# Transposing attention probabilities as two halves of 64 query rows, on the two row halves of TensorE and into two PSUM banks

## The reference

```python
q = l2norm(q) * qs; k = l2norm(k) * ksc
q, k = rotary_xpos(q, k)
sim = jnp.einsum('bhwid,bhwjd->bhwij', bq * 8.0, look_around(bk))   # i: 128 queries, j: 256 keys
sim = jnp.where(mask, -jnp.finfo(sim.dtype).max, sim)
attn = jax.nn.softmax(sim, axis=-1)
out = jnp.einsum('bhwij,bhwjd->bhwid', attn, look_around(bv))
x = x + o @ wo                                                      # then a gated feed-forward block
```

## Time and profile before

| | |
|---|---|
| median of 3 runs | 2342.65 us (2342.46 to 2345.71) |
| span of the profiled execution | 2341.2 us; no other time is given for that execution |
| TensorE matmuls busy | 2090.4 us (89%) |
| weight loads busy | 1569.1 us (67%) |
| DVE, ACT, POOL busy | 1155.5, 930.8, 652.2 us |
| mean granted TensorE clock | 0.938 |
| local attention, first to last score | 586.05 to 1212.4 us, with a feed-forward block between its layers |

### The profile page before, as it was taken

How to read it: one execution, slowest core, us unless ns; L and a number is a source line. 1 busy time by engine, 2 the same in 40 slices (tenths; PEclk the granted TensorE clock), 3 DMA queues, 4 the chain that set the end, 5 groups by cost and what they waited for, 6 DMA issues and landing times. The chain is left out here.

```text
span 2341.2 us, 38218 instructions
## 1 busy us (share of the span) xinstructions
PE 2090.4 (89%) x12396; PEld 1569.1 (67%) x12396; DVE 1155.5 (49%) x4116; ACT 930.8 (40%) x2973; POOL 652.2 (28%) x568
## 2 busy tenths in 40 slices
PE   8996899776999989899989979979997799599998
PEld 5764488554667745467764558758886577489997
DVE  4886244365777732377763347722221465423332
ACT  3652132233666632266663125412221466133332
POOL 0377556522122210022211002222223022213332
PEclk8997799978999999899999979979998899699999
DMA  6601299875920020100000072111220801372221
GB/s 228 267 16 35 93 322 341 234 246 160 343 104 10 9 62 0 38 10 10 10 12 1 1 257 97 36 42 31 35 38 10 288 28 35 139 253 37 36 35 19
DMA packets 155370, 232.21 MB, mean 99 GB/s; under 512 B 36585, under 2 KB 123604, under 8 KB 154262
## 3 DMA queue, kind: packets, MB, share of 16 engines
q1 hardware_dynamic: 125750, 201.55, 24.7%
q0 software_dynamic: 29424, 28.21, 6.8%
HBM read 142.88 MB, written 101.04 MB: 104 GB/s over the span
## 5 line engine op out<-in xcount | busy, mean ns | idle before, releaser
L3058 POOL TENSOR_TENSOR la_invnorm<-la_clamped,all_minushalf 128x16 f32<-128x16 f32 x32 | 92.9, 2903 | 372.7 <-DVE la_clamped L3123 372.7
L2679 ACT ACTIVATE m3e_ht<-m3e_h_bank,m3w_b 128x128 f32<-128x128 f32 x312 | 89.1, 369 | 188.8 <-PE m3e_h_bank L2652 188.8
L3205 ACT ACTIVATE la_probs<-la_probs,la_nb,la_invnorm 128x256 f32<-128x256 f32 x256 | 150.1, 591 | 5.1 <-DVE la_nb L3145 5.1
L2652 PE MATMUL m3e_h_bank<-m3e_xt,m3e_w 128*128 128x128 f32 x1248 | 147.4, 277 | 0.0
L2624 POOL DMA_INDIRECT out<-m3e_y,m3e_dest x39 | 82.0, 2102 | 225.4 <-DVE m3e_y L2724 223.4
L2652 PEld LDWEIGHTS m3e_h_bank<-m3e_xt,m3e_w 128*128 128x128 f32 x1248 | 144.3, 194 | 0.1
L2663 PE MATMUL m3e_y_bank<-m3w_w,m3e_ht 128*128 x624 | 141.0, 379 | 0.0
L881 POOL DMA_INDIRECT m_xbuf<-m0w_rows,m0w_slots x128 | 127.8, 998 | 37.5 <-issue 36.0
L2843 ACT ACTIVATE m2e_ht<-m2e_h_bank,m2w_b 128x270 f32<-128x270 f32 x128 | 62.2, 487 | 178.7 <-PE m2e_h_bank L2808 178.6
L2783 POOL DMA_INDIRECT m_sum<-m2e_y,m2e_dest x48 | 70.2, 1463 | 199.3 <-DVE m2e_y L2891 193.8
L2663 PEld LDWEIGHTS m3e_y_bank<-m3w_w,m3e_ht 128*128 128x128 f32 x624 | 115.7, 190 | 14.1
(11 more groups left out here) (486 smaller groups left out, 4806.0 us busy)
## 6 DMA issues: line engine op xcount, KB each, us to landing
m0w_wgu<-in_m_gu SPq DMA_DIRECT2D x32, 768.0 KB, 10.0
m_xbuf<-all_zeros SPq DMA_DIRECT2D x38, 528.0 KB, 5.9
m3e_w<-in_m_w SPq DMA_DIRECT2D x17, 1024.0 KB, 5.0
m2w_w<-in_m_w SPq DMA_DIRECT2D x16, 1024.0 KB, 12.6
m0e_wd<-in_m_down SPq DMA_DIRECT2D x32, 384.0 KB, 11.1
m_xbuf<-all_zeros SPq DMA_DIRECT2D x16, 576.0 KB, 6.4
m0w_xb<-m_xbuf SPq DMA_DIRECT2D x32, 288.0 KB, 8.2
m_sum<-all_zeros SPq DMA_DIRECT2D x16, 512.0 KB, 7.2
```

The lines of the kernel that those rows point to most:

```text
L2652: last = nc.tensor.matmul(h_ps[t % 2][half][:, i * R:(i + 1) * R], w1[t % NW][:, c, f0:f0 + P], xt[t % 2][:, c, :], start=c == 0, stop=c = ...
L2679: last = nc.scalar.activation(h_t[t % 2][:, 4 * half + i, :], h_ps[t % 2][half][:, i * R:(i + 1) * R], m.act, bias=ahead.b1[:, bass.ds(e * ...
L3058: nc.gpsimd.tensor_tensor(inv_norm[t % 2][:, :], clamped[t % 2][:, :], k.minus_half[:, :], ALU.pow).then_inc(powered.sem, 1)
L3205: last = nc.scalar.activation(probs[u][:, hh, :], probs[u][:, hh, :], ACT.Exp, bias=nb[u][:, hh:hh + 1], scale=inv_norm[u][:, hh:hh + 1], ...
```

## The change

The 128 x 128 blocks are no longer transposed whole. Each is cut into two halves of 64 query rows; a half is loaded as a stationary operand on its own 64 rows of the array and multiplied by the 64x64 corner of the identity on the same rows. The half of queries 0 to 63 goes to one bank and that of queries 64 to 127 to the next, in alternation, so that banks 0 and 1 together hold heads 0 to 3, and banks 2 and 3 heads 4 to 7. The exponentials are awaited in twos, the last two of 16 transposes of a group signal the two banks, and each of ScalarE's four copies now takes four heads' halves, in runs of 64 columns, in place of two whole heads. The counts of the semaphores stay.

```diff
+QH = P // 2
...
                 def copy_p(t):
                     u = t % 2
                     act.wait_ge(mixed.sem, mixed.at(t - 2, "mixed"))
-                    for j, (h0, h1) in enumerate(SCORE_BANKS):
+                    for j in range(4):
+                        h0, q0 = 4 * (j // 2), QH * (j % 2)
                         act.wait_ge(p_turned.sem, p_turned.at(t, f"{j}"))
-                        nc.scalar.copy(probs_t[u][:, h0:h1 + 1:2, :, :].rearrange("p h w n -> p h (w n)"),
-                                       score_ps[j][:, :].rearrange("p (h n) -> p h n", h=2)).then_inc(p_copied.sem, 1)
+                        nc.scalar.copy(probs_t[u][:, h0:h0 + 4, :, q0:q0 + QH].rearrange("p h w n -> p (h w) n"),
+                                       score_ps[j][:, :].rearrange("p (h n) -> p h n", n=QH)).then_inc(p_copied.sem, 1)
...
                 def turn_p(t):
-                    for j, pair in enumerate(SCORE_BANKS):
-                        pe.wait_ge(exped.sem, exped.at(t, f"{j}"))
-                        for i, hh in enumerate(pair):
+                    for j0 in (0, 2):
+                        pe.wait_ge(exped.sem, exped.at(t, f"{j0 + 1}"))
+                        for i in range(4):
                             for w in range(2):
-                                c0 = i * 2 * P + w * P
-                                last = nc.tensor.transpose(score_ps[j][:, c0:c0 + P], probs[t % 2][:, hh, w * P:(w + 1) * P], k.ident[:, :])
-                        last.then_inc(p_turned.sem, 1)
+                                for half in range(2):
+                                    q0, c0 = QH * half, (2 * i + w) * QH
+                                    last = nc.tensor.transpose(score_ps[j0 + half][:, c0:c0 + QH], probs[t % 2][q0:q0 + QH, 2 * j0 + i, w * P:(w + 1) * P],
+                                                               k.ident[q0:q0 + QH, q0:q0 + QH])
+                                    if i == 3 and w == 1:
+                                        last.then_inc(p_turned.sem, 1)
```

## The result

The changed kernel takes 2349.64 us (median of 20 runs, 2344.37 to 2357.12) against 2342.65 us (20 runs): a ratio of 1.0026, 95% interval 1.0018 to 1.0034, which is 6 us or 0.26% slower. (The two medians are 7.0 us apart; the means, 2349.86 and 2343.86 us, are 6.0 apart, and the ratio follows them.) A second measurement of both gave 1.0019 (1.0005 to 1.0034). That lies inside the range on record, above the range of the likeliest case (to 2346.5), and on the other side of the 0.2% line: "slower", to which the prediction gave 0.22, and not "same", to which it gave 0.72.

The account below looks back on a forecast made before the run. The ring through ScalarE, POOL and DVE bounds regular tiles at 15.08 us; a 0.22 us delay against 0.21 spare gives 0.01 x 28 = 0.3 us, so 2343.0 us, with 80% and more between 2341.0 and 2353.0.

Parts of the forecast that it names:

- the likeliest case: Whole kernel: "same", no difference beyond 0.2% (4.7 us), with its own range of 2341.5 to 2346.5 us; chance 0.72.
- The ring: Regular tiles: a closed chain from scores to next scores through ScalarE, POOL and DVE, 15.09 us, without turn_p and mix.
- TensorE is the bound: Rival for regular tiles: saved transpose time comes off each tile, 28 x 0.55 = 15 us, giving 2327; chance 0.05.
- (a): Probability transposes in turn_p: 0.064 us per pair of halves; the 16 pairs take about 1.0 us, 0.7 less.
- main rival for "slower": In turn_p halves do not run side by side or drain between each other: 10 us more, 2353; chance 0.20.
- (b): Between project and turn_p the array's division changes: 0.10 us added, and 0.05 for the first pair after.
- (c): Banks 0 and 1 are ready together after eight pairs, so the first copy and mix start 0.22 us later.
- D: Delay of the first copy, and so of mix, in a tile: 0.22 us, against 0.21 to spare.
- (d): ScalarE's copies in runs of 64 columns: no cost taken, 2.8 us the most allowed.
- (e): Exponentials awaited in twos: costs nothing in regular tiles, and nothing in the last tile of a layer.
- The rival by the clock: Regular tiles: TensorE idles about 0.7 us more, one slow stretch per tile costs up to 48 us; chance 0.03.
- three signs of being wrong: The ring contains something turn_p touches, the pair pace is above 0.087 us, or the granted clock falls below 1.00.

Follow-up runs that it names:

- e1: The changed kernel, but the last tile of each layer has its probabilities transposed whole, as before; ratio 0.9997 to the kernel before.
- e3: The changed kernel, but within a group all halves of queries 0 to 63 come first, then those of 64 to 127; ratio 1.0028 to the kernel before.
- e4: The kernel before, but 8 of 16 probability transposes are left out of every tile; ratio 1.0024 to the kernel before.
- e6: The changed kernel, but within a group the halves of each two heads await only those heads' exponentials; ratio 1.0021 to the kernel before.
- e7: The kernel before, but in each layer's last tile the whole transposes await the exponentials in twos, as in the changed kernel; ratio 0.9997.
- e10: The changed kernel, but in each layer's last tile every half transpose is made twice into the same place; ratio 0.9998 to the kernel before.

## Why the prediction was right or wrong

*The bound.* Right. The ring through ScalarE's exponentials, POOL's power and DVE's product sets a regular tile, and TensorE's transposes are not on it: 211.1 us for 14 tiles in the kernel after and in e1, e3, e4 and e6 alike, with turn_p between 1.0 and 1.9 us. The rival "TensorE is the bound" fell with e4.

*(a) The pace of a pair.* Right: (1.22 - 0.226) / 31 = 0.032 us an instruction, 0.064 a pair, as taken. The halves do run side by side, so the main rival for "slower" fell; the kernel is slower for another reason.

*(b) The changes of shape.* The first transpose starts 9.24 us after the scores (706.72 - 697.48) instead of 9.14: 0.10, as taken.

*(c) Later copies, later mix.* The first copy starts 10.04 us after the scores instead of 9.84: D = 0.20, where 0.22 was worked out, and mix moved by the same (708.74 - 697.48 = 11.26 against 11.05). The key transposes follow the query ones with no wait for DVE left, and the tile did not grow. (d) A copy takes 0.59 us and four take 2.05, as before: no cost.

*(e) The last tile.* This is the step that failed. It asked only when the copies are due, and found nothing: indeed mix starts 8.27 us after the scores in both kernels. It did not ask what the halved work does to the clock where TensorE waits between the bursts, and booked the last tile at 0 us; there mix alone lost 1.59 and 1.39 us at the lower clock. The rival by the clock had the right mechanism in the wrong place: it was weighed for a regular tile, which is 92% busy now and had 1.00, and was given 0.03 and a price of up to 48 us. Of the prediction's three signs of being wrong, the one that came is the last, a granted clock below 1.00. The last tile needed its own look: TensorE worked there in four bursts of 0.66 us with pauses of 0.5 us between them, and the change left two bursts of 0.7 us, 1.62 apart.

That the time lies inside the range on record is luck. The room above 2346.5 us was there for halves that do not overlap, which did not happen, and the prediction says itself that its range leaves the clock out.

*The size.* In the last tile 1.59 and 1.39 us of mix are lost. What follows changes too, up to the end of the feed-forward block: in layer 2 the stretch in the table is 152.8 to 153.1 us in all six profiles with a slow mix, and 148.6 to 150.6 in the six with a fast one and the old place of turn, so 2.2 to 4.5 us with mix's 1.4 included. The granted clock of this stretch is 0.93 in all six with a slow mix and 0.95 to 0.97 in the other six; in the first profiles of before and after:

```profile
1210.62:1359.58 148.96, 135.52 (x500) 77.96 (x500) 58.50 (x161) 36.68 (x78) 9.82 (x17) 0.97 0.01 2
1214.76:1367.66 152.90, 138.56 (x516) 80.44 (x516) 58.49 (x161) 36.66 (x78) 9.78 (x17) 0.93 0.01 2
```

So the fall in mix is followed by more time at the lower clock in the feed-forward block. In layer 1 the stretch from the last tile's scores to the first scores of layer 2 is 166.3 to 166.8 us in before, again before, e1, e7 and e10, and 167.0 to 167.2 in five of the six profiles with a slow mix: most of the 1.6 us of mix is made up again behind it. In the sixth, the second profile of the kernel after, it is 170.2. The two layers add up to 2.4 to 8.4 us, which holds the 6 us measured, but the usual case is 2.4 to 5.4, a little short of it.

The mean granted clock of each timed run points the same way without any profile. Averaged over the runs of a kernel it is 0.9333 to 0.9348 in the five with a slow mix, the kernel after among them, and 0.9368 to 0.9376 in before, e1, e7 and e10. On one chip the difference to before is 0.002 to 0.004. As an estimate, that share of 2345 us is 5 to 9 us of matmul work at full clock, if TensorE worked all through the stretches at the lower clock. How the 6 us divide among mix and the stretches behind it stays open.

What the rows show of the clock is which of the two levels held in a stretch. That the amount of TensorE's work ahead of mix decides which one it is there is shown by e10 against the kernel after, by e7 against e6, and by e4; what measure of work counts is not shown (e3). The Trainium skill, page "TensorE: Matmul & The Clock Gate", section "Part 4: PE-mode transpose", says of a transpose that "it doesn't count as PE-busy the same way". This case does not bear that out for its float32 transposes: in e10 more of them alone take mix from a granted clock of 0.53 to 1.00.

## What to carry to other kernels

Before costing a saving on an engine, find the ring that sets one step of the loop, and the room of the side branch against each engine of it: here 0.21 us read from one timeline predicted the cost of 1.75 us of added work to 0.01 us a tile. A saving off that ring is worth nothing, and on TensorE it can cost: look for the places where it already works in short bursts (first and last tiles, pipeline drains), since less work there can halve its clock for what comes next, as it did in mix of the last tiles (0.53 instead of 1.00). The price of the edges has to be worked out apart from that of the steady state.

## What was not expected of the hardware

Float32 transposes on alternating row halves, each with its own weight load of 128 columns, run at 0.032 us an instruction. Issued in runs of eight on one half (e3) they still overlap where the half changes: 32 take 1.63 us, where 0.06 each would give 31 x 0.06 + 0.23 = 2.1. And in e4, with eight transposes fewer in every tile, the granted clock of the 32 matmuls of mix in the last tile was 0.54 and not 1.00, while the regular tiles kept their 15.08 us.
